# Block-sparse layer of a four-layer attention chain: both masks of the scores in one tile, and the exp of the turned scores masked by a minimum on VectorE

## The reference

```python
scores = jnp.einsum('bhqd,bhkd->bhqk', q, kh) / jnp.sqrt(jnp.float32(D))
block_repr = k.reshape(B, nb, BLOCK, D).mean(axis=2)
r = jax.nn.relu(block_repr @ r_w1.T + r_b1) @ r_w2.T + r_b2
keep0 = jax.nn.sigmoid(r[0, :, 0]) > 0.5
allowed = keep0[:, None] & keep0[None, :]
allowed_pos = jnp.repeat(jnp.repeat(allowed, BLOCK, 0), BLOCK, 1)
scores = jnp.where(allowed_pos[None, None], scores, NEG)
causal = jnp.triu(jnp.ones((S, S), bool), k=1)
scores = jnp.where(causal[None, None], -jnp.inf, scores)
p = jax.nn.softmax(scores, axis=-1)
out = jnp.einsum('bhqk,bhkd->bhqd', p, vh)
```

## Time and profile before

| | |
|---|---|
| median of the runs | 400.49 us (3 runs, 400.41 to 402.63) |
| the profiled execution | 399.31 us |
| its span (first to last instruction) | 397.5 us |
| TensorE busy | 345.6 us (87% of the span) |
| VectorE busy | 225.3 us (57%) |
| ScalarE busy | 197.0 us (50%) |
| GpSimd busy | 91.0 us (23%) |
| mean granted TensorE clock | 0.977 of full speed |

### The profile page before, as it was taken

One profiled execution on the slowest core, in us unless ns is written; L12 is line 12 of the kernel. 1 busy time (PEld: TensorE's weight loads), 2 busy tenths in 40 slices (PEclk: granted clock), 3 DMA queues, 4 the chain that ended last, 5 costly groups with the idle time before them and its releaser, 6 DMA issues.

```text
span 397.5 us, 9351 instructions
## 1 busy us (share of the span) xinstructions
PE 345.6 (87%) x3749; PEld 221.6 (56%) x3749; DVE 225.3 (57%) x445; ACT 197.0 (50%) x419; POOL 91.0 (23%) x277
## 2 busy tenths in 40 slices
PE   5988989984999999998798999889888999899891
PEld 2424556663777878877453545445555665556551
DVE  6243485267476666769444334465566536546754
ACT  1544556553676768666323333433645363454550
POOL 7042443110000001000035213122334133232321
PEclk9999999996899999999899999999999999999997
DMA  7390000000000000000000100000010000000000
GB/s 241 119 405 11 2 2 3 2 0 0 2 0 2 2 2 0 2 2 29 26 2 0 54 8 35 26 3 15 35 35 15 2 15 5 12 15 9 21 15 28
DMA packets 7451, 11.96 MB, mean 30 GB/s; under 512 B 2024, under 2 KB 4464, under 8 KB 7152
## 3 DMA queue, kind: packets, MB, share of 16 engines
q1 hardware_dynamic: 6720, 10.04, 7.2%
q10 hardware_dynamic: 688, 1.32, 0.9%
HBM read 6.63 MB, written 0.52 MB: 18 GB/s over the span
## 4 chain that ended last, share of the span: by engine, by line
PE 68%; DVE 11%; ACT 10%; issue 8%; DMA 1%; POOL 1%; POOLq 0%; SPq 0%; ACTq 0%
PE psum L286 16%; PE psum L344 8%; PE psum L660 5%; PE psum L321 4%; PE psum L569 4%; PE psum L295 3%; PE psum L685 3%; PE psum L711 3%; ACT probs L760 3%; PE psum L719 2%; PE psum L636 2%; PE psum L309 2%; PE psum L696 2%; DVE mres L815 2%; PE psum L357 2%
## 5 line engine op out<-in xcount | busy, mean ns | idle before, releaser
L468 DVE TENSOR_REDUCE maxs<-psum 128x8 f32<-128x1024 f32 x64 | 78.3, 1225 | 93.2 <-PE psum L309 36.2
L394 ACT ACTIVATE probs<-psum 128x1024 f32<-128x1024 f32 x64 | 65.6, 1025 | 109.4 <-PE psum L321 109.4
L286 PE MATMUL psum<-km,qT 32*128 32x512 f32 x256 | 71.4, 638 | 20.8 <-ACT xnT L560 6.5
L295 PE MATMUL psum<-qm,kT 32*128 32x512 f32 x256 | 72.1, 638 | 0.7 <-ACT probs L394 0.7
L286 PEld LDWEIGHTS psum<-km,qT 32*128 32x128 f32 x256 | 20.1, 183 | 35.7 <-issue 20.3
L760 ACT ACTIVATE probs<-psum,maxs 128x128 f32<-128x128 f32 x128 | 35.0, 396 | 3.3 <-DVE maxs L805 3.3
L321 PEld LDWEIGHTS psum<-mrow,sel 32*128 32x128 bf16 x512 | 19.0, 93 | 31.6 <-issue 29.7
L344 PE MATMUL psum<-probs,vpad 128*32 128x128 f32 x1024 | 34.4, 275 | 0.0
L527 POOL TENSOR_SCALAR rstd<-stats 128x2 f32<-128x2 f32 (+1 forms) x18 | 4.1, 226 | 128.8 <-DVE stats L495 128.8
L444 POOL CAST mp<-maxs 128x16 bf16<-128x16 f32 x32 | 6.8, 213 | 113.5 <-DVE maxs L468 113.5
L344 PEld LDWEIGHTS psum<-probs,vpad 128*32 128x32 f32 x1024 | 27.0, 110 | 10.1 <-issue 8.3
(11 more groups left out here) (152 smaller groups left out, 627.4 us busy)
## 6 DMA issues: line engine op xcount, KB each, us to landing
km<-kT SPq DMA_DIRECT2D x30, 64.0 KB, 1.9
wmat<-in_wmat SPq DMA_DIRECT2D x1, 1856.0 KB, 11.6
qm<-qT SPq DMA_DIRECT2D x16, 64.0 KB, 1.9
wmat<-in_wmat SPq DMA_DIRECT2D x1, 1024.0 KB, 7.5
qm<-qT SPq DMA_DIRECT2D x32, 32.0 KB, 1.8
wrow<-in_wrow SPq DMA_DIRECT2D x1, 704.0 KB, 5.3
ctxT<-in_ctxt SPq DMA_DIRECT2D x2, 256.0 KB, 5.0
xnT<-in_xt ACTq DMA_DIRECT2D x2, 256.0 KB, 6.4
```

What stands on the lines that cost most here:

```text
L286: s_mm = e.matmul(bank(j), qT[rg(j), bt(b)], km[L.slot][rg(j), :, bt(b)], start=True, stop=L in (LC, L3), skip_group_check=True)
L295: e.matmul(bank(4 + a), kT[rg(j), M.slot, bt(b)], qm[rg(j), :, bt(b)], start=True, stop=False, skip_group_check=True)
L394: e.activation(probs_of(n, half), bank(4, 2), ACT.Exp, scale=layer(n).scale)\
L468: e.tensor_reduce(maxs[:, n % 2, 8 * half:8 * half + 8], bank(2 * half, 2).rearrange("p (h k) -> p h k", k=P), AX.X, ALU.max, negate=True)\
```

## The change

Three things change in L2's self attention.

1. **S** gets one mask. The tile causal[:, 0] now also holds the block mask, added once; so the block-mask matmuls of S go and the causal matmul stays.
2. **T** gets no mask. Instead its exp, 128 keys x (8 heads x 128 queries) in SBUF, is limited by a minimum on VectorE with the tile causal[:, 1], which holds 0 where a score is masked and 3e38 where it isn't. There are two minima per item (`dve_past`), and `pe_V` waits for them instead of the exp.
3. The block mask is built on GpSimd from `keep` and a per-partition copy of it, `kmine`; the tiles blkA, blkB and keepr go.

```diff
@@ pe_scores
-            if n is not None and L in (L0, L2):
+            if n is not None and L is L0:
...
                 for a in range(2):
                     s_mm = S_more(e, n, half, a)
-                if L is L0:
-                    s_mm.then_inc(sem("S_mm"), 1)
-            if m is not None and M in (L0, L2):
+                s_mm.then_inc(sem("S_mm"), 1)
+            if m is not None and M is L0:
                 for a in range(2):
                     T_more(e, m, mhalf, a)
...
             if m is not None:
-                if M is L2:
-                    for a in range(2):
-                        e.matmul(bank(4 + a), identB[:, :], causal[:, 1, :].unsqueeze(1).broadcast_to([P, 4, P]),
-                                 start=False, stop=False, skip_group_check=True)
@@ pe_V
-            e.wait_ge(sem("exp_done"), 2 * n + 2)
+            if layer(n) is L2:
+                e.wait_ge(sem("past_only"), 2 * (n - B) + 2)
+            else:
+                e.wait_ge(sem("exp_done"), 2 * n + 2)
@@ new on VectorE
+        def dve_past(e, n, half):
+
+            p8 = probs_of(n, half).rearrange("p (h q) -> p h q", q=P)
+            if n == B and half == 0:
+                e.wait_ge(sem("masks"), 8)
+            e.wait_ge(sem("exp_done"), 2 * n + half + 1)
+            e.tensor_tensor(p8, p8, causal[:, 1, :].unsqueeze(1).broadcast_to([P, 8, P]), ALU.min)\
+             .then_inc(sem("past_only"), 1)
@@ dve_attn
                 if n is not None:
                     dve_max(e, n, 0)
+                if n2 is not None and layer(n2) is L2:
+                    dve_past(e, n2, 0)
                 even(s)
                 if n3 is not None:
                     dve_norm(e, n3)
                 if n4 is not None:
                     dve_z(e, n4)
+                if n2 is not None and layer(n2) is L2:
+                    dve_past(e, n2, 1)
                 if n is not None:
                     dve_max(e, n, 1)
                 odd(s)
@@ GpSimd, before the steps of L2
+            m = sem("masks")
+            e.wait_ge(sem("keep"), 1)
...
+            e.tensor_tensor(kother[:, 0, :], keep[:, :], one, ALU.subtract).then_inc(m, 1)
+            e.tensor_tensor(kother[:, 1, :], mine, one, ALU.subtract).then_inc(m, 1)
+            e.wait_ge(m, 2)
+            e.tensor_tensor(kblk[:, 0, :], kother[:, 0, :], mine, ALU.mult).then_inc(m, 1)
+            e.tensor_tensor(kblk[:, 1, :], kother[:, 1, :], keep[:, :], ALU.mult).then_inc(m, 1)
+            e.wait_ge(m, 4)
+            e.tensor_scalar(kother[:, 0, :], kblk[:, 0, :], -NEG, None, ALU.mult).then_inc(m, 1)
+            e.tensor_scalar(kother[:, 1, :], kblk[:, 1, :], 1.0, None, ALU.add).then_inc(m, 1)
...
+            e.wait_ge(m, 6)
+            e.tensor_tensor(halves(causal[:, 0, :]), halves(causal[:, 0, :]), wide(kother[:, 0, :]), ALU.add)\
+             .then_inc(m, 1)
+            e.tensor_tensor(halves(causal[:, 1, :]), halves(causal[:, 1, :]), wide(kother[:, 1, :]), ALU.mult)\
+             .then_inc(m, 1)
@@ TensorE, L1's place (7, 2)
-                    e.wait_ge(sem("blocks"), 4)
-                    e.wait_ge(sem("causal"), 2)
+                    e.wait_ge(sem("masks"), 7)
@@ VectorE, L1's places (6, 0) and (6, 1)
-                    e.tensor_scalar(keepr[:, 0, :], keep[:, :], group[:, 0:1], group[:, 1:2], ALU.mult, ALU.add)\
-                     .then_inc(t, 1)
...
-                    e.tensor_scalar(keepr[:, 0, :], group[:, 1:2].broadcast_to([P, 2]), 2.0 * NEG, None, ALU.mult)\
-                     .then_inc(sem("negs"), 1)
...
+                    e.tensor_copy(kmine[0:BLOCK, 0:1], keep[0:BLOCK, 0:1]).then_inc(sem("kmine"), 1)
+                    e.tensor_copy(kmine[BLOCK:P, 0:1], keep[BLOCK:P, 1:2]).then_inc(sem("kmine"), 1)
```

55 lines of the change are left out of this document (24 added, 31 removed).

## The result

| | before | after |
|---|---|---|
| median of the runs | 400.45 us (measured beside it) | 388.12 us (4 runs, 387.02 to 389.39) |
| ratio, 95% interval | | 0.9687 [0.9654, 0.9719] |
| profiled execution, span | 399.31, 397.5 us | 389.39, 387.6 us |
| TensorE busy | 345.6 us | 333.5 us |
| VectorE busy | 225.3 us | 241.7 us |

The kernel is 3.1% faster.

What follows compares the result with a forecast made beforehand. TensorE was taken to set the pace. Its savings of 12.3 + 1.0 + 0.8 = 14.1 us less VectorE's 4.0 gave 10.1: 389.2 us profiled, 390.4 as median, range 386.2 to 394.6.

Steps and rivals of the forecast that it cites:

- mrow's wait: L2 steps: TensorE's 0.76 us idle for ScalarE's copy mrow follows exp and T, so it moves forward whole.
- Rival D: L2 steps: waits on ScalarE's exp and mrow set the step; only 1.0 + 0.8 us gained, 398.7; chance 0.04.
- forecast signs: Signs expected in the trace if right, among them V waiting for a minimum in steps 12, 14 and 16.
- T's halves: Sixteen half steps with T of L2: each saves 0.77 us (block pairs 0.33, T's causal pair 0.44), 12.3 us.
- Halves with S alone: Three halves at L2's start lose only the block pair, 0.33 us each: 1.0 us saved.
- The end of L1: Without small VectorE instructions the maximum starts sooner; gain limited to ScalarE's idle time before its exp, 0.8 us.
- GpSimd's eight instructions: End of L1: building the mask on GpSimd takes 2.2 us, done before TensorE needs it, so hidden.
- Minima of 1.22 us: VectorE in L2: each of sixteen minima takes 1.22 us, like same-size rows, 19.5 us in all.
- Rival C: VectorE: a minimum costs two passes, 2.4 us, so VectorE becomes the bound; 407 us; chance 0.03.
- VectorE's losses: Steps 12 to 17: minima delay V or a projection's add that TensorE waits for, giving back 4.0 us.
- rival A: L2: VectorE not in the way, 386.4 us, or the clock also stays up (1.5 us), 384.9; chance 0.18.
- Rival B: Steps 11 to 17: VectorE and GpSimd hold each other up, 0.77 us per step, 5.4 in all; 395.8; chance 0.13.

Runs made afterwards that it cites:

- Run 4: Changed kernel with the causal mask pair of S issued ahead of the fp32 score matmuls instead of behind them: 387.26 us, ratio 0.9664.
- Run 10: Changed kernel with two unused VectorE instructions put back at the end of L1, like those the change took out: 392.28 us, ratio 0.9793.
- run 1: Changed kernel with VectorE's minima left out, so masked weights stay in V's input: 386.20 us, ratio 0.9643.
- run 6: Changed kernel with each item's first minimum moved to the end of the step before, behind the second row maximum: 386.09 us, ratio 0.9633.
- run 11: Changed kernel with six tiny GpSimd operations (adds, copies or memsets) beside the first minimum in steps 11, 12 and 14: 388.24 us, one execution.
- run 8: Run 7's kernel plus twelve fp32 matmuls that nobody reads in TensorE's idle time at the end of L1: 385.98 us, ratio 0.9613.
- run 7: Changed kernel with the first minimum a step early and S's causal pair ahead of the fp32 scores: 384.39 us, ratio 0.9586.

## Why the prediction was right, and where it was off

**What bounds it, and that mrow's wait moves: right.** TensorE sets the pace; the wait of 0.76 stands in step 12 unchanged. Rival D (only 1.8 us gained) fell. Of the forecast signs one did not come: V waits for a minimum in step 16 (0.50 us), but not in steps 12 and 14.

**T's halves, 16 x 0.77 = 12.3: mis-sized, 11.0.** Of the sixteen halves the thirteen that have S of L2 too save 0.65 (step 11: 8.39 - 7.09 = 1.30 for two). I priced what stays, one causal pair, from its place behind the block pair. Now it stands directly behind the fp32 scores, which run in bands of 32 rows, and it starts 1.08 us after the half's start where the block pair started at 0.96. Run 4, with the pair ahead of them, took that 0.12 back. The three halves with LC's S have no pair that stays, so the row maxima follow the scores, and they save 0.86. 13 x 0.65 + 3 x 0.86 = 11.0.

**Halves with S alone, 1.0: mis-sized, 0.63.** Same cause: in the second and third of them the causal pair starts 1.06 us after the scores instead of 1.28, so 0.22 sooner and not 0.33. The first, at half clock, gained 0.38 so (1.94 to 1.56), but of that 0.20 was left at the second one's start, since the eight L1 matmuls between them took 1.78 us instead of 1.62.

**The end of L1, 0.8: 0.90 measured.** The reasoning (ScalarE's idle time is the limit) held: the exp now follows ScalarE's own copy. Run 10 gives back about half of it; the other half is what L1402 took longer beside a memset than its like in run 10.

**GpSimd's eight instructions, hidden: right**, though they took 3.1 us (182.13 to 185.24) and not 2.2, one of them 1.38.

**Minima of 1.22 us: right** (median 1.214). Rival C fell with it.

**VectorE's losses, 4.0: mis-sized, 3.3.** Forecast and measured (the last two columns of the table): step 12 0.27 and 0, 13 0.88 and 0.83, 14 0.27 and 0, 15 1.09 and 0.82, 16 0.67 and 0.71, 17 0.86 and 0.95. The minima end nearly where I laid them (the second of step 12 at 227.71 + 1.19 - 222.48 = 6.42 us, forecast 6.35). But V in step 12 starts at 6.49 with them and without (run 1): TensorE itself comes there no sooner, and not at 6.23, for the 0.24 us that its two halves gained less. Of the same error one term took what the other gave: steps 12 and 14 came out to 0.03 us. Runs 1 and 6 show that these losses are the minima's and their order's, so the part of rival A by which nothing is lost fell.

**Sum.** 14.1 - 4.0 = 10.1 forecast; 11.0 + 0.6 + 0.9 - 3.3 = 9.2 from the traces, and 0.7 that happened to come ahead of the change. Without that 0.7 the profiled execution would have taken 390.1, not 389.4. The medians differ by 12.3, more than either: the profiled execution before was 1.1 below its median, the one after 1.3 above. Of executions without a trace only the mean granted clock is known, and it has a part in this. The changed kernel's profiled execution had 0.978; the other three, 1.1 to 2.4 us faster, had 0.981 to 0.984. Of 34 executions of the kernel before that ran beside the experiments, 22 at 0.974 to 0.978 took 399.4 to 400.9 us, and 12 at 0.968 or 0.969 took 402.2 to 403.1. Where in the kernel their clock fell is not known. In the trace of the changed kernel it is at 0.57 for four us around 195, as before; in that of run 11, whose steps are the same, it is at full:

```profile
191.00:201.00 10.00, 8.88 (x70) 5.36 (x71) 4.97 (x7) 2.43 (x4) 1.28 (x6) 1.00 0.02 7
```

Its D is 1.65 us shorter, close to the 1.5 that rival A took. The idle time ahead is 1.93 us in both. So the shorter idle time doesn't settle the clock. Of the eleven traces with about 1.93 us there (all but before, run 8, whose idle time is filled, and run 10), seven kept full clock around 195 and four did not; the two with more (2.83 before, 2.40 in run 10) did not, and two are too few to say that they can't. All four with the mask pair first kept it, and three of the other seven, also too few to say whether that order has a part in it. How often it stays up in executions without a trace is open.

**Rival B: real as a mechanism, nothing as a price.** Its holds are in the trace after, off the path: from the first T matmul to step 11, where GpSimd held up a minimum, it is 11.95 us with the minima and without, and steps 14 and 18, behind the held rstd of steps 13 and 17, last as long as in run 1 (7.51 and 6.22 us), as does step 16 up to its second scores (3.20 us). In runs 6 and 7 the holds are on the path.

## What to carry to other kernels

Lay each new instruction out on its engine from the step's start: what waits behind it decides, not its total (19.5 us of minima cost 3.3, and 0.0 in steps where nothing waited behind them). When matmuls go, price the ones that stay in their new neighbourhood, not the old. When an instruction with two SBUF operands comes to VectorE, look at what GpSimd reads in the same microsecond, and whether TensorE waits for it.

## What the runs showed of the hardware

**VectorE and GpSimd.** In the changed kernel GpSimd's first step of rstd, usually 0.23 us, took 1.10 in steps 13, 15 and 17, each time to the end of the minimum beside it:

```profile
235.87 1.19 DVE L471 TENSOR_TENSOR probs<-probs,causal 128x1024 f32<-128x1024 f32 x1
...
236.04 1.10 POOL L533 TENSOR_SCALAR rstd<-stats 128x2 f32<-128x2 f32 x1 [4.38 <-DVE stats L497]
```

In step 10 it was the other way round: two minima that started at 209.40 took 3.31 us together, beside an add of GpSimd over 128x512 that had started first.

```profile
208.01 2.49 POOL L520 TENSOR_TENSOR resid<-x,wrow 128x512 f32<-128x512 f32 x2
...
209.40 3.31 DVE L471 TENSOR_TENSOR probs<-probs,causal 128x1024 f32<-128x1024 f32 x2
```

The row maximum, whose operand is in PSUM, held nothing up: GpSimd's cast L445 took its usual 0.20 us beside the one at 263.08. The Trainium skill (SBUF — State Buffer, "Who interferes with whom") says that a VectorE instruction with two SBUF inputs contends with a GpSimd instruction that reads SBUF and not with one that only writes. The trace agrees: run 11's adds and copies were held to 1.1 and 1.2 us, its memsets took 0.1. L1402 with its 0.79 us beside a memset is another case. It reads one SBUF operand and the memset reads none, so the sentence on two inputs doesn't cover it, and in run 10 the like instruction came ahead of the memset.

**The clock.** After the same idle time of 1.93 us TensorE's clock fell to its lower level, 1.2 GHz, in some executions and not in others, and cost 1.65 us where it fell (changed kernel against run 11). After 1.44 us in step 10 it stayed up in the changed kernel and fell in run 10 (1.6 us), though in both traces it had fallen around 195 us as well; in run 7 it fell after idle times of 1.12 and 0.96 close together. An edit that moves idle time can so be worth 1.6 us more or less than its rows say, and only the trace of that execution tells which.
